# A decoder layer with eight experts: expert rows scattered to token order while the experts run, contiguous loads in the last stage, and 71 tiles with written-out programs

## What is computed

```python
scores = softmax(xf @ Wg.T)
expert_weights, expert_indices = top_k(scores, 2)
expert_weights = expert_weights / expert_weights.sum(-1, keepdims=True)
h1 = xf @ W1[e].T + low-rank part + b1[e]
h3 = xf @ W3[e].T + low-rank part + b3[e]
g = silu(h1) * h3
y_e = g @ W2[e].T + low-rank part + b2[e]
y = sum over the two chosen e of gate[e] * y_e
x = layernorm(x + y)
```

## Time and profile before

| what | value |
|---|---|
| median of 3 runs | 1605.15 us (1604.17 to 1608.46) |
| the profiled execution | 1601.91 us, of which the profile's span covers 1600.1 us |
| busy in the span: PE / DVE / ACT / POOL | 83% / 55% / 50% / 41% |
| mean granted TensorE clock | 0.905 of full speed |
| stage `route_and_merge` | from 960.7 us to 1060.1 us |
| stage `experts` | from 1060.4 us to 1494.1 us |
| stage `combine` | from 1494.07 us to 1600.1 us |

### The profile page before, as it was taken

One profiled execution on the slowest core, in us unless ns is written; L12 is line 12 of the kernel. 1 busy time (PEld: TensorE's weight loads), 2 busy tenths in 40 slices (PEclk: granted clock), 3 DMA queues, 4 the chain that ended last, 5 costly groups with the idle time before them and its releaser, 6 DMA issues. The chain is left out here.

```text
span 1600.1 us, 20916 instructions
## 1 busy us (share of the span) xinstructions
PE 1334.3 (83%) x6346; PEld 605.8 (38%) x6347; DVE 885.2 (55%) x1325; ACT 794.6 (50%) x911; POOL 655.6 (41%) x449
## 2 busy tenths in 40 slices
PE   3988379999999999994999964989999999999200
PEld 1434112222222222222455533646666666666100
DVE  1323268888888888881454536644433434443355
ACT  1666069999999999991665530012222222222000
POOL 0323057777777777772433402111111111111475
PEclk7999779999999999996999875799999999999655
DMA  3888682454246234214211009611111111111243
GB/s 113 263 284 297 187 299 67 111 146 156 71 113 229 67 78 115 72 39 115 80 66 54 1 2 318 238 51 43 46 45 43 46 46 46 44 45 40 81 134 113
DMA packets 119643, 176.00 MB, mean 110 GB/s; under 512 B 11090, under 2 KB 80375, under 8 KB 119031
## 3 DMA queue, kind: packets, MB, share of 16 engines
q1 hardware_dynamic: 111062, 155.99, 31.5%
q0 software_dynamic: 6528, 17.83, 3.9%
q10 hardware_dynamic: 1984, 1.30, 0.3%
HBM read 114.66 MB, written 60.42 MB: 109 GB/s over the span
## 5 line engine op out<-in xcount | busy, mean ns | idle before, releaser
L489 DVE TENSOR_TENSOR sa_probs<-sa_sum,sa_strips 128x1024 f32<-128x1024 f32 x352 | 413.3, 1219 | 93.2 <-PE sa_sum L441 72.9
L531 POOL TENSOR_TENSOR sa_probs<-sa_probs,sa_factors 128x1024 f32<-128x1024 f32 x160 | 381.1, 2382 | 152.5 <-ACT sa_probs L507 125.1
L513 ACT ACTIVATE sa_probs<-sa_probs 128x1024 f32<-128x1024 f32 (+1 forms) x256 | 341.3, 1373 | 7.9 <-DVE sa_probs L489 7.9
L453 PE MATMUL sa_o<-sa_probs,sa_v 128*32 128x512 f32 x2048 | 273.5, 606 | 2.8 <-POOL sa_probs L531 2.3
L1880 PE MATMUL xp_ps_h<-w,arena 128*128 x576 | 261.1, 596 | 1.2 <-ACT arena L1934 1.1
L441 PE MATMUL sa_sum<-sa_q,sa_k 97*128 97x512 bf16 x704 | 199.4, 387 | 32.2 <-DMA sa_v<-vpad 23.3
L1860 POOL DMA_INDIRECT arena<-x_rows,token_of x72 | 68.4, 950 | 383.8 <-PE xp_ps_x L1872 336.7
L1934 ACT ACTIVATE arena<-xp_ps_x 128x256 f32<-128x256 f32 x72 | 27.6, 383 | 379.8 <-PE xp_ps_x L1872 379.8
L1976 DVE TENSOR_TENSOR arena<-xp_ps_h,ffn_b 128x1024 f32<-128x1024 f32 x72 | 88.2, 1225 | 182.6 <-PE xp_ps_h L1880 182.6
L507 ACT ACTIVATE sa_probs<-sa_factor 128x1024 f32<-128x1024 f32 x160 | 163.1, 1020 | 44.6 <-PE sa_factor L441 44.6
L441 PEld LDWEIGHTS sa_sum<-sa_q,sa_k 97*128 97x128 bf16 x704 | 48.5, 98 | 273.5 <-DVE sa_probs L489 199.1
(11 more groups left out here) (208 smaller groups left out, 1415.6 us busy)
## 6 DMA issues: line engine op xcount, KB each, us to landing
sa_strips<-line SPq DMA_DIRECT2D x4, 3840.0 KB, 19.4
qstack<-qp_parts SPq DMA_DIRECT2D x96, 128.0 KB
kstack<-qp_parts SPq DMA_DIRECT2D x96, 128.0 KB, 2.0
sa_q<-qstack SPq DMA_DIRECT2D x16, 768.0 KB
sa_k<-kstack SPq DMA_DIRECT2D x16, 768.0 KB
table_y<-xp_y SPq DMA_DIRECT2D x72, 128.0 KB, 1.7
vpad<-qp_v_out SPq DMA_DIRECT2D x16, 512.0 KB, 3.4
sa_v<-vpad SPq DMA_DIRECT2D x16, 512.0 KB
```

The source lines that it names most:

```text
L453: last = nc.tensor.matmul(ps_o[n % 2][32 * h:32 * h + 32, :], v[m % 2][:, jt, 32 * h:32 * h + 32], probs[s % RING][:, h, :], start=(jt == ...
L489: nc.vector.tensor_tensor(probs[s % RING][:, 2 * half:2 * half + 2, :], ps_sum[sums_before(s, half) % 2][:, :, :], strips[hg % 2][:, 2 * h ...
L513: nc.scalar.activation(probs[s % RING][:, 0:heads, :], probs[s % RING][:, 0:heads, :], ACT.Exp, scale=0.25).then_inc(exp_done, 1)
L531: nc.gpsimd.tensor_tensor(probs[s % RING][:, 2:4, :], probs[s % RING][:, 2:4, :], factors[hg % 2][:, :, c1 - CH:c1][:, :, ::-1], ALU.mult) ...
```

## The change

1. **71 tiles.** NT becomes 71.
2. **Scatter during the experts.** The place numbers of the one-hot matmuls become 1 to 8192 (`numbers`, first choices 1 to 4096, second 4097 to 8192), so the same PSUM result tells the token and which choice it is. Six small VectorE steps in place of one make `token_of` and `place_of` from it; lanes without a token get a place in 256 spare rows (`dump`). `rows` and its cast go. One more constant is loaded. SP no longer stores `y`: POOL scatters each tile's 128 rows to `y_places` (first choices, then second, in token order), in the same queue as the gathers, each scatter five tiles behind the gather that stands before it.
3. **Written-out programs.** The loop in `pipeline` is a Python loop, so TensorE, ScalarE and VectorE run straight code in `experts`; so does `combine`.
4. **The last stage.** SP loads both choices of a chunk with two plain DMAs from `y_places` (512 KB each, four chunks ahead); ScalarE multiplies with the gates (8 operations per chunk) and normalises (4, as scale and offset); VectorE does two sums of 128x1024 in place of eight fused operations of 128x256, and no longer normalises; POOL has a third small operation (`offset`).

```diff
-NT = T * 2 // P + E_
+NT = T * 2 // P + E_ - 1
...
-            step(nc.vector.tensor_copy(rows[:, :, :], place[:, :, :]))
...
-            step(nc.vector.tensor_copy(token_of[:, :],
-                                       ps_c[0][:, :, :].rearrange("p t e -> p (t e)")[:, 0:NT]))
+            number = ps_c[0][:, :, :].rearrange("p t e -> p (t e)")[:, 0:NT]
+            step(nc.vector.tensor_scalar(second_choice[:, :], number, T + 0.5, -float(T), ALU.is_gt, ALU.mult))
+            step(nc.vector.scalar_tensor_tensor(out=found[:, :], in0=number, scalar=-1.0, in1=second_choice[:, :],
+                                                op0=ALU.add, op1=ALU.add))
+            step(nc.vector.tensor_scalar(token_of[:, :], found[:, :], 0.0, None, ALU.max))
+            step(nc.vector.scalar_tensor_tensor(out=empty[:, :], in0=number, scalar=0.5, in1=dump[:, :],
+                                                op0=ALU.is_lt, op1=ALU.mult))
+            step(nc.vector.scalar_tensor_tensor(out=found[:, :], in0=number, scalar=-1.0, in1=empty[:, :],
+                                                op0=ALU.add, op1=ALU.add))
+            step(nc.vector.tensor_copy(place_of[:, :], found[:, :]))
...
         def pipeline(eng, head, body, tail):
             head()
-            with eng.Fori(0, LOOPED // 2) as pair:
-                for i in range(2):
-                    body(2 * pair + 1 + i, 1 + i)
+            for s in range(1, NT - 3):
+                body(s, s % 2)
             tail()
...
+            def scatter(s):
+                pool.wait_ge(y_done, 1 + s + 1)
+                pool.indirect_dma_start(out=io["y_places"], out_offset=bass.IndirectOffsetOnAxis(place_of[:, s:s + 1], 0),
+                                        in_=y[s % 2][:, :], in_offset=None).then_inc(y_stored[s % 2], 16)
+
+            for s in range(NT + 5):
+                if s < NT:
+                    gather(s)
+                if s >= 5:
+                    scatter(s - 5)
...
+            def load(c):
+                for n, dst in enumerate((ya, yb)):
+                    rows = io["y_places"][n * T + c * CH:n * T + (c + 1) * CH, :]
+                    sp.dma_start(dst[c % RING][:, :, :], rows.rearrange("(t p) d -> p t d", p=P)
+                                 ).then_inc(loaded[c % RING], 16)
+
+            for c in range(RING):
+                load(c)
+            for c in range(NCH):
+                if c + RING < NCH:
+                    sp.wait_ge(summed, c + 1)
+                    load(c + RING)
+                sp.wait_ge(normed, c + 1)
+                sp.dma_start(io["out"][c * CH:(c + 1) * CH, :].rearrange("(t p) d -> p t d", p=P),
+                             out[c % 2][:, :, :]).then_inc(stored[c % 2], 16)
...
+            def weight(c):
+                act.wait_ge(loaded[c % RING], 32 * (c // RING + 1))
+                for n, y in enumerate((ya, yb)):
+                    for t in range(TT):
+                        last = nc.scalar.activation(y[c % RING][:, t, :], y[c % RING][:, t, :], ACT.Copy,
+                                                    scale=weights[:, n, c * TT + t:c * TT + t + 1])
+                last.then_inc(weighted, 1)
+
+            def normalise(c):
+                act.wait_ge(offset_done, c + 1)
+                for t in range(TT):
+                    last = nc.scalar.activation(out[c % 2][:, t, :], out[c % 2][:, t, :], ACT.Identity,
+                                                bias=offset[c % 2][:, t:t + 1], scale=rstd[c % 2][:, t:t + 1])
+                last.then_inc(normed, 1)
+
+            weight(0)
+            for c in range(NCH):
+                if c + 1 < NCH:
+                    weight(c + 1)
+                normalise(c)
...
+                dve.wait_ge(weighted, c + 1)
+                added = counted_step(nc.vector.tensor_tensor(ya[c % RING][:, :, :], ya[c % RING][:, :, :],
+                                                             yb[c % RING][:, :, :], ALU.add))
+                if c >= 2:
+                    dve.wait_ge(stored[i], 16 * (c // 2))
+                dve.wait_ge(dve_done, added)
+                nc.vector.tensor_tensor(out[i][:, :, :], ya[c % RING][:, :, :], x2_all[:, c * TT:(c + 1) * TT, :],
+                                        ALU.add).then_inc(summed, 1)
```

More of the change, by code:

```diff
@@ L1841, in _, with gather @@
                          bass.AP(io["b2"].tensor, 0, [[0, P], [1, E_ * D]])).then_inc(b2_loaded, 16)
[L1843 to L1851, removed]
             for i in range(2):
-                sp.wait_ge(y_stored[i], 1 + 16 * NT // 2)
+                sp.wait_ge(y_stored[i], 16 * ((NT + 1 - i) // 2))
         @block.gpsimd
         def _(pool):
-            for s in range(NT):
+            def gather(s):
                 if s >= 2:
@@ L2016, in sem @@
             return ctx.enter_context(nc.semaphore("co_" + name))
[L2018 to L2019 removed]
+        RING = 4
+        ya = [sb(f"ya{i}", [P, TT, D]) for i in range(RING)]
+        yb = [sb(f"yb{i}", [P, TT, D]) for i in range(RING)]
         out = [sb(f"out{i}", [P, TT, D]) for i in range(2)]
@@ L2029, in combine, with _ @@
+        exponent_set, weighted, summed, dve_done, var_done, rstd_done, offset_done, normed = (
+            sem(n) for n in ("exponent_set", "weighted", "summed", "dve_done", "var_done", "rstd_done", "offset_done",
+                             "normed"))
         stored = [sem(f"stored{i}") for i in range(2)]
         block = ctx.enter_context(nc.Block())
+        @block.sync
+        def _(sp):
+            def load(c):
[12 more added lines that the diff above has]
+                             out[c % 2][:, :, :]).then_inc(stored[c % 2], 16)
+            for i in range(2):
+                sp.wait_ge(stored[i], 16 * NCH // 2)
@@ L2032, in _ @@
         @block.gpsimd
         def _(pool):
-            def gather(c):
+            pool.wait_ge(exponent_set, 1)
+            for c in range(NCH):
+                i = c % 2
+                pool.wait_ge(var_done, c + 1)
                 if c >= 2:
-                    pool.wait_ge(summed, TT * (c - 1))
-                for t in range(TT):
-                    for n, dst in enumerate((ya, yb)):
-                        pool.indirect_dma_start(
-                            out=dst[c % 2][:, t, :], out_offset=None, in_=io["table_y"],
-                            in_offset=bass.IndirectOffsetOnAxis(rows[:, n, c * TT + t:c * TT + t + 1], 0)
-                        ).then_inc(gathered[c % 2], 16)
@@ L2095, in _ @@
-        @block.sync
-        def _(sp):
-            with sp.Fori(0, NCH // 2) as pair:
-                for i in range(2):
-                    c = 2 * pair + i
-                    sp.wait_ge(normed, TT * (c + 1))
-                    sp.dma_start(io["out"][bass.ds(c * CH, CH), :].rearrange("(t p) d -> p t d", p=P),
-                                 out[i][:, :, :]).then_inc(stored[i], 16)
-            for i in range(2):
-                sp.wait_ge(stored[i], 1 + 16 * NCH // 2)
+                    pool.wait_ge(normed, c - 1)
```

165 lines of the change are left out of this document (72 added, 93 removed).

## The result

The changed kernel takes 1558.41 us (median of four runs, 1555.46 to 1560.55); the kernel before, run beside it, 1605.78 (four runs). The ratio is 0.9708, with a 95% interval of 0.9689 to 0.9727. The forecast was 1555.5, 1548 to 1566. The gain is 47.4 us by the medians, where 49.6 was summed. A second measurement of the same code gave 1556.52 against 1603.9, again 47.4.

The account below looks back on a forecast made before the run. TensorE bounds `experts`, POOL's queue of gathers `combine`. Routing 0.45 - 0.2, one tile less -5.8, last scatter +1.0 and `combine` -45.0 sum to -49.6, so 1605.15 us becomes 1555.5, range 1548 to 1566.

Parts of the forecast that it names:

- `experts` is TensorE's own work: In `experts`, TensorE waits for nobody; one tile less saves 5.8 us, scatters and straight code cost nothing per tile.
- Routing: Routing stage: one more constant costs +0.45 us, the dropped cast of `rows` gives -0.2, five small steps cost 0.
- The five small steps: End of routing: 1.3 us of added VectorE steps cost 0, hidden in its 1.62 us wait for TensorE's first product.
- The cover: End of routing: VectorE's 1.62 us wait for TensorE's first product hides the added steps; without it they cost 1.3 us.
- The last scatter: End of `experts`: a scatter lands in 2.7 us where the direct store took 1.7, so +1.0 us before the barrier opens.
- The ring: In `combine`, VectorE, POOL and ScalarE wait in turn, ScalarE weighting chunk c+2 only after normalising c: 11.6 us per two chunks.
- pointers cost ScalarE nothing: Rival, `combine`: ScalarE spacing 0.29 us, 10 us per two chunks, stage 54.4 us, kernel 1549 us; chance 0.08.
- The end: End of `combine`: the last store and the end after chunk 7's normalising take 4.1 us, as before the change.
- The sums shut POOL out: Rival, `combine`: POOL waits out VectorE's two-SBUF sums, 4.0 for 1.7 us, 3.6 to 4 late by chunk 7; 1559.5 us; chance 0.22.
- as summed: Whole kernel: the forecast's terms hold without a rival, 1553 to 1558 us; chance 0.50.
- the forecast's row of times: In `combine`, VectorE starts the even chunks at 8.9, 20.5, 32.0 and 43.5 us after the barrier.

## Why the prediction was right, point by point

**`experts` is TensorE's own work: right.** Steps of 5.82 with and without scatters, with and without loops, and 5.74 for a tile in the pair of kernels that differ in one. The scatter was taken from the gather's rows as 0.94 on POOL and 2.7 to landing; it is 0.99 and 2.4.

**Routing: +0.25 forecast, +0.8 to +1.1 measured.** VectorE's first step comes 5.58 us after the stage's first issue (4.84 before), +0.74 for the constant where +0.45 was summed; in the thirteen executions with this code it is 5.43 to 6.61. The five small steps are hidden as said: VectorE's wait for the first product fell from 1.62 to

```profile
1022.52 0.69 DVE L1790 TENSOR_TENSOR w<-ro_m,w 128x512 f32 x1 [0.35 <-PE ro_m L1671]
```

and the way from the first step to this sum is 52.62 us (52.91 before). The cover was there, and 0.35 is left of it. From this sum to the first issue of `experts` it is 42.55 us (41.88 before), +0.67 that no term of the forecast had; in the thirteen executions this part is 41.51 to 42.94, so it is no effect that these runs show.

**The last scatter: +1.0 forecast, +1.9 measured.** The issue comes 0.25 later and the landing takes 0.73 longer, together what was forecast. The term that failed is the barrier, which was taken to cost the same after either: from landing to `combine` it is 1.67 us instead of 0.73, because POOL's own drain ends last.

**The ring: right.** Forecast 4.6 + 1.7 + 2.0 + 3.2 + 0.1 = 11.6, measured 4.75 + 1.72 + 1.98 + 3.31 = 11.76. VectorE's first sum came 8.94 us after the barrier (forecast 8.9), chunk 7's 5.15 after chunk 6's (5.1). ScalarE's spacing is 0.40 and 0.49 (0.39 and 0.48), so "pointers cost ScalarE nothing" falls. The kernel with four output chunks shows that the order and not a buffer closes it, and the one two chunks ahead that opening it alone leads into the next.

**The end: 4.1 us forecast, 3.4 measured** (the last normalising ends at 1555.0).

**The sums shut POOL out: the rival was half right.** Its working for chunk 0 (4.0 us where 1.7 was) came out as 3.45, from 1509.17 to the normalising at 1512.62, where the later chunks take 1.72: 1.7 us late. From the earlier trace rows, a gather beside such sums, I had taken that nothing changes in the sum; that was the mis-sized term: the gather was 0.3 us longer, the power 1.01. What the rival had wrong is what came later: in chunks 2, 4 and 6 ScalarE releases VectorE's next sum only when POOL's power is already under way (1522.94, sum at 1523.07), and then neither is longer, 1.01 and 1.23; only the last small operation waits for the sum's end, 0.33 for 0.20. In the odd chunks no sum runs beside POOL's three operations. So the cost is 1.7 us once and 0.13 in each of three turns, not 4. By the prediction's own bands the measured 1558.4 stands just outside "as summed" (1553 to 1558) and in this rival's (1558 to 1562), although the rival's mechanism gave only the 1.7. Without any of it the stage is 60.57, and the forecast for that case was 61.0.

**Together.** For `combine`: 61.0 + 1.7 (POOL at chunk 0) + 0.7 (three turns of 11.76 or 11.77, where the forecast's row of times, 8.9 to 43.5, had 34.6 for the three) - 0.7 (the end) + 0.2 (0.15 of it VectorE's last chunk) = 62.9, as measured. That the stage came within 2 us is in part luck: a delay that was left out and an end that was put too long were of opposite sign. In the profiled executions the stages miss the forecast by 1.7 to 1.9 here, 0.9 in the passage, 0.5 to 0.9 in the routing and 0.1 to 0.6 in `experts`; the medians miss it by 2.2, and the difference lies within what the code ahead of the routing varies.

## What to carry to other kernels

When a change takes the bound of a stage away, work out the ring that is left, engine by engine, and see which engine stands in it twice: here moving arithmetic to an idle engine cost 5 us, although it lightened the busy one. Behind a ring closed by the order of work a second one closed by a buffer can lie, so order and buffers have to be opened together: 0 and 1 us apart, 8 together. Small operations on POOL that others wait for are kept clear of VectorE sums with two SBUF operands by putting one operand in PSUM, which cost nothing here.

## What the runs showed of the hardware that I had not expected

- The shutting out was one-sided here: a POOL operation that comes while a two-SBUF sum runs waits for that sum's end (0.20 becomes 1.03, 1.01 becomes 2.02), while a sum that comes while POOL's 1.01 us power runs starts and ends on time. Beside VectorE's operations of 128x256, 0.48 us each, POOL's two take 0.37 and 1.13, which would fit a wait for the one under way but was not tested. The section of the Trainium skill named above calls the shared ports an exclusive lock; of VectorE's side of such a lock these rows show nothing. Whether a POOL operation that reads more than 4 numbers per partition would delay a sum, no run here shows.
- A block that ends after scatters of POOL takes 2.17 us longer to hand over (4.36 against 2.19), whether or not an engine waits for them by semaphore: POOL's drain ends 1.35 us after the last one has landed.
- Code that is the same in every kernel took between 960.25 and 966.60 us up to the routing, more than most effects studied here.
